# Attention phase of a vision block on one core: scores for the maxima six pairs ahead, maxima turned at step 1, query copies issued in the odd chunks

## The reference, cut to what matters

```
attn_w = softmax(einsum('bhqnd,bhknd->bhnqk', qh, kh) + mask_w)
vw     = einsum('bhnqk,bhknd->bhnqd', attn_w, vh)
attn_h = softmax(einsum('bqwnd,bkwnd->bwnqk', qh, kh) + mask_h)
out    = einsum('bwnqk,bknwd->bqwnd', attn_h, vw)
```

## Time and profile before

| what | value |
|---|---|
| median of 3 runs | 2617.39 us |
| the profiled execution, its own time | 2628.1 us |
| its span | 2626.3 us (1.8 us lie around it) |
| attention phase in the span | about 444 to 1888 us |
| PE / DVE / ACT / POOL busy over the span | 84% / 57% / 47% / 40% |
| mean granted clock of PE | 0.91 of full |
| DMA, mean rate | 133 GB/s |
| mean of one: `exps` / `line_max` / `normalise` (two parts) | 0.54 / 0.62 / 0.51 and 0.63 us |

### The profile page before, as it was taken

How to read it: one execution, slowest core, us unless ns; L and a number is a source line. 1 busy time by engine, 2 the same in 40 slices (tenths; PEclk the granted TensorE clock), 3 DMA queues, 4 the chain that set the end, 5 groups by cost and what they waited for, 6 DMA issues and landing times. The chain is left out here.

```text
span 2626.3 us, 85046 instructions
## 1 busy us (share of the span) xinstructions
PE 2196.2 (84%) x31886; PEld 1742.7 (66%) x31886; DVE 1490.1 (57%) x2350; ACT 1238.4 (47%) x2079; POOL 1061.6 (40%) x1661
## 2 busy tenths in 40 slices
PE   6977515988888898897898989989779984999998
PEld 6977513656666666665666666666579983777777
DVE  3677874656556565554565666666431213677675
ACT  2444531534444444453454544444334554666665
POOL 2344554434444344433444444444312233433433
PEclk9988755989989999887998999999889996999999
DMA  6575536665666666667666666666396753444442
GB/s 106 114 173 154 154 113 143 154 133 132 140 141 143 147 135 143 141 146 166 147 153 146 148 150 149 157 150 161 69 142 124 159 128 101 96 96 94 95 95 68
DMA packets 716326, 348.34 MB, mean 133 GB/s; under 512 B 613481, under 2 KB 675137, under 8 KB 716097
## 3 DMA queue, kind: packets, MB, share of 16 engines
q1 hardware_dynamic: 686993, 314.26, 53.7%
q0 software_dynamic: 28800, 30.58, 4.0%
q10 hardware_dynamic: 304, 0.03, 0.0%
HBM read 105.39 MB, written 102.76 MB: 79 GB/s over the span
## 5 line engine op out<-in xcount | busy, mean ns | idle before, releaser
L693 ACT ACTIVATE att_prob<-att_st_ps 128x448 f32<-128x448 f32 x896 | 487.2, 544 | 674.4 <-PE att_st_ps L585 673.0
L768 DVE TENSOR_REDUCE att_mm<-att_s_ps 128x8 f32<-128x448 f32 x896 | 548.6, 621 | 263.0 <-PE att_s_ps L552 262.0
L598 PEld LDWEIGHTS att_pv_ps<-att_vx,att_prob 128*56 128x56 f32 x14336 | 543.6, 137 | 141.4 <-issue 18.6
L598 PE MATMUL att_pv_ps<-att_vx,att_prob 128*56 128x18 f32 x14336 | 510.8, 205 | 1.8 <-ACT att_prob L693 1.8
L580 PE MATMUL att_st_ps<-att_mvt,att_both 122*56 122x448 bf16 x1792 | 341.0, 376 | 161.9 <-DMA att_mvt<-att_mneg 116.3
L552 PE MATMUL att_s_ps<-att_kx,att_q_unit 120*56 120x448 bf16 x1792 | 335.9, 371 | 5.7 <-DMA att_q_unit<-att_qk_hi 3.2
L585 PE MATMUL att_st_ps<-att_qx,att_k_hi 128*56 128x448 bf16 x1792 | 339.6, 374 | 0.0
L585 PE MATMUL att_st_ps<-att_qx,att_k_lo 128*56 128x448 bf16 x1792 | 336.6, 371 | 0.0
L430 POOL COPY att_vx<-att_vf 56x224 f32<-56x224 f32 x512 | 182.0, 386 | 306.8 <-PE att_pv_ps L598 298.3
L445 POOL DMA_DIRECT2D att_mvt<-att_mneg x256 | 135.8, 535 | 307.8 <-PE att_st_ps L585 232.6
L436 POOL DMA_DIRECT2D att_qx<-att_q_hilo x512 | 245.0, 487 | 26.9 <-DMA att_q_hilo<-att_qk_lo 15.8
(11 more groups left out here) (207 smaller groups left out, 3283.3 us busy)
## 6 DMA issues: line engine op xcount, KB each, us to landing
att_xt<-xn_chunks SPq DMA_DIRECT2D x128, 196.0 KB, 3.6
att_k_hi<-att_qk_hi SPq DMA_DIRECT2D x128, 196.0 KB, 3.8
att_k_lo<-att_qk_lo SPq DMA_DIRECT2D x128, 196.0 KB, 4.1
att_qx<-att_q_hilo POOLq DMA_DIRECT2D x512, 49.0 KB, 3.0
pos_x<-in_x_dram SPq DMA_DIRECT2D x128, 105.0 KB, 3.6
lepe_x<-v_scratch SPq DMA_DIRECT2D x128, 105.0 KB, 3.0
x_scratch<-pos_x SPq DMA_DIRECT2D x128, 98.0 KB
xn_chunks<-pos_xrt SPq DMA_DIRECT2D x16, 784.0 KB, 4.9
```

The lines of the kernel that those rows point to most:

```text
L598: ins = pe.matmul(pv_ps[v % 2][64 * h:64 * h + L, at:at + 18], prob[t % 4][:, 4 * h + a, :], vx[v][:, VW * j + 36 * a + 18 * h:VW * j + 36 ...
L693: act.activation(prob[t % 4][:, :, :], st_ps[t % 2][:, 0:S8].rearrange("p (s q) -> p s q", q=L), ACT.Exp).then_inc(exp_done, 1)
L768: dve.tensor_reduce(mm[v % 2][:, NH * j:NH * j + NH], s_ps[j % 2][:, 0:S8].rearrange("p (s k) -> p s k", k=L), AX.X, ALU.max).then_inc(max ...
```

## The change

Three constants move the work of PE, ACT and DVE by steps: the plain scores run 6 pairs ahead instead of 4, the maxima are turned at step 1 instead of 3, and the two halves of the projection are at steps 0 and 1 instead of 1 and 2. On SP the two `q_hilo` DMAs leave `copies` of the even chunk and follow `keys_and_units` in the odd chunk before. On POOL `fill_max` goes ahead of `fill_k`, on DVE the first `line_max` of a chunk goes ahead of `normalise`. No instruction of a chunk is added or removed, apart from one more wait on SP.

```diff
-        S_EARLY = 4
-        MAXIMA_AT = 3
-        PROJECT_AT = (1, 2)
+        S_EARLY = 6
+        MAXIMA_AT = 1
+        PROJECT_AT = (0, 1)
...
-            def copies(i, w):
+            def queries(i, w):
 
                 wait(sp, qk_low, cnt(i, 2 * w + 1, 2, 2))
                 wait(sp, qx_in[w], unit_count(i, 16 * NH, -16 * NH))
                 sp.dma_start(q_hilo[w][0:C, :], qk_hi[w][0:C, :]).then_inc(hq_in[w], 16)
                 sp.dma_start(q_hilo[w][C:2 * C, :], qk_lo[w][0:C, :]).then_inc(hq_in[w], 16)
+
+            def keys_twice(i, w):
+
+                wait(sp, qk_low, cnt(i, 2 * w + 1, 2, 2))
                 wait(sp, st_done, cnt(i, 2 * w + 1, 7, 7 - 28))
                 for y in range(2):
                     sp.dma_start(k_hi2[w][C * y:C * y + C, :], qk_hi[w][C:2 * C, :]).then_inc(k2_in[w], 16)
...
                     if is_there(*n4):
                         keys_and_units(n4[0], w)
+                        queries(n4[0], w)
                 else:
                     n2 = chunk(i, v, 2)
                     if is_there(*n2):
-                        copies(n2[0], 1 - w)
+                        keys_twice(n2[0], 1 - w)
...
-                if v % 2 and is_there(*n4):
-                    fill_k(pool, n4[0], w, K_POOL, kx_in_sw)
                 if is_there(*n1):
...
                     fill_max(*n1)
+                if v % 2 and is_there(*n4):
+                    fill_k(pool, n4[0], w, K_POOL, kx_in_sw)
...
                 for j in range(PAIRS):
-                    if j == 0 and not is_first(i, v):
-                        normalise(*chunk(i, v, -1))
                     if j < PAIRS - S_EARLY:
                         if is_there(*n1):
                             line_max(*n1, j + S_EARLY)
                     elif is_there(*n2):
                         line_max(*n2, j - (PAIRS - S_EARLY))
+                    if j == 0 and not is_first(i, v):
+                        normalise(*chunk(i, v, -1))
```

More of the change, by code:

```diff
@@ L354, in first @@
                 keys_and_units(i, 0)
-                copies(i, 0)
+                queries(i, 0)
+                keys_twice(i, 0)
                 sp.wait_ge(x_mask, 1)
@@ L367, in first @@
                 keys_and_units(i, 1)
+                queries(i, 1)
                 store_v(i, 2)
```

## The result

| | before | changed |
|---|---|---|
| median, us (lowest to highest) | 2619.28 (2617.33 to 2640.52) | 2506.49 (2504.56 to 2513.52) |
| ratio, with 95% interval | | 0.9556 [0.9519, 0.9593] |
| profiled execution, us / its span | 2628.1 / 2626.3 | 2513.52 / 2511.6 |
| mean granted clock of TensorE | 0.912 | 0.927 |

The medians are of four runs each; the 2617.39 us given for the kernel before at the start is the median without the highest, 2640.52. The change gains 112.8 us; 98 had been forecast (2521 us, range 2486 to 2578). Lines of the changed kernel are 7 higher than before from the attention code on: L587 is the `mvt` matmul that was L580, L592 the keys' matmuls, L559 the scores, L567 `maxima`, L521 the projection, L687 `high`, L693 `negate`, L452 `fill_max`.

The account below looks back on a forecast made before the run. PE's waits for the maxima DMA at even chunk ends were taken as the bound. Columns 72 us plus rows 29, less three late POOL turns at 1.1, gave about 98: median 2519, stated as 2521 us, range 2486 to 2578.

Parts of the forecast that it names:

- What bounds the kernel: PE before the transposed scores: waits for the maxima DMA at the end of even chunks, near 1.8 us each.
- the "issue" waits: PE at row borders: 43.8 us in 11 waits of about 4 us, taken as the hardware loop's turn and staying.
- The working of the new chunk: Step times from the border: negate behind high, 4.05 to 4.31 us; first maxima DMA at 5.07 us, against 6.55 before.
- L552's wait for `neg_done`: PE at step 2: scores pair 1 waits for the negation, adding 0.17 us to each chunk, bounds 0 and 0.5.
- The residual wait of an even chunk: PE's remaining wait for the maxima DMA at even borders: 0.3 us per even chunk in both halves, bounds 0 and 1.2.
- The late turns of POOL: Three column borders where PE lost near 4 us behind a late POOL: 1.1 us of each stays.
- The clock: TensorE's low clock follows border waits: columns counted at 1.00; rows keep a 2.5 us loss per image behind the loop turn.
- The first: Rival: maxima DMA slower as transfers pack closer, 1.2 us per even border instead of 0.3; 2578 us, chance 0.15.
- The third: Rival: q_unit becomes the wait at step 1 of every even chunk; at a 2 us stall 2693 us, chance 0.04.
- The fourth: Rival: the column loop begins to pay at its turn like the row loop; 79 us lost, 2600, chance 0.03.
- The second: Rival, better than forecast: no residual wait and no wait for neg_done; 133 us gained, 2484 us, chance 0.13.
- The query copies: SP's q_hilo DMAs: 392 KB leave the saturated even chunk, counted as no gain.

Follow-up runs that it names:

- the two pairs of runs: Query copies in the even chunk against the odd one: 2509.12 and 2506.49 us with the POOL swap, 2517.68 and 2516.37 us without it.
- the best version: The changed kernel with negate ahead of high on ACT and PE's row loop written out: 2408.06 us, ratio 0.9169 against the kernel before.

## Why the prediction was right, and where it was short

- **What bounds the kernel: right.** The wait for the maxima at the end of even chunks was the cost that the change removes; the turn of the row loop was not, and stayed. The prediction took the "issue" waits for the loop's turn and left 53 us out of the gain for it; the changed kernel has all 13, and writing the loop out removes them. Its guess that two of the "DMA" waits by rows were turns is right too: their places and lengths (4.07 and 4.06 us) say so. The Trainium skill (Runtime: NRT & Kernel Launch, Instruction fetch mechanics) says the same of a taken branch outside the prefetched pages. That it was the fetch inside the turn is only argued; that it is the turn is shown.
- **The working of the new chunk: right.** `negate` behind `high` ended 4.28 us in (worked out 4.31), the DMA left at 5.06 (5.07). The 1.2 us lost behind `high` are real: `negate` ahead of `high` brings 23 us back.
- **The term that was too large: L552's wait for `neg_done`**, taken at 0.17 us for each chunk. In the changed kernel the scores of pair 1 start at 1053.72, 4.33 us in, 0.05 us behind the end of `negate`. PE's own work brings it there at 4.30 (so it is in the run with `negate` first, where nothing holds it: 1409.06 for a border at 1404.76), and not at 4.23: the step with `maxima` and a projection is 1.85 us in the trace (step 1, 1404.92 to 1406.77), where 1.76 had been worked out. So the wait is 0.03 to 0.05 us, not 0.17. With four chunks an image that is some 0.5 us an image, or 15 us over 30 images.
- **The residual wait of an even chunk** was taken at 0.3 us. By columns it is 5.9 us over some 31 even chunks, 0.19. By rows it is 8.8 us in 15 waits, 0.6 each and twice the forecast: there the transfer took 5.2 us in the median of these waits, against the 4.8 that the prediction took from one chunk. The two halves cancel.
- **The late turns of POOL** were to keep 1.1 us each, three by columns. No column border waits over 1.2 us now. POOL still pauses, but in another place, see below. That is 3 us.
- Taken together: column image 37.33 us, forecast 38.0; row image 45.21, forecast 45.6. (0.67 + 0.39) x 15 = 16 us, and with the 3 us of POOL 19; the profiled spans gained 17 us more than the forecast of 98, the medians 15. By columns the 0.67 is 0.5 of `neg_done` and 0.2 of the two even waits. By rows the 0.39 is 0.5 of `neg_done` and 0.3 of the turn (49.5 / 13 = 3.8 us, forecast 4.1), less 0.3 for the even wait. The figure 2521 itself is 2 us above the 2519 of the prediction's own sum, for which it gives no reason.
- **The clock: right for the columns**, 1.00 in every image of that view. PE was busy 41.0 us less in all, with the same instructions. The low clock followed PE's waits at the borders: where they are gone, so is it; by rows, with the loop's turn left, it stayed at 0.95 in the image shown, and it is 1.00 up to 1030 us once the loop is written out.
- **Rivals.** The first, a slower maxima DMA, has a true core: 5.54 against 4.81 us in the row chunk shown, and it cost 0.6 us there. It did not come to 1.2 us per even chunk. The third, `q_unit`, was as near as the prediction put it: in the even chunk by columns that begins at 1403.41 it is issued at 1402.43, lands 2.5 us later and is needed at 1406.22, a cover of 1.3 us. 1.1 us later on SP costs 69 us of waits and as much in time. In the changed kernel it is waited for in 7 places, 5.8 us, of which 3.1 are one wait at the start of the phase. The fourth did not happen: the columns have no wait called "issue", though each image between the first and the last ones turns the loop. The second came true by half.
- **The query copies** were counted at nothing, which was right (1.3 and 2.6 us in the two pairs of runs, within the noise); that they'd be worth 10 to 30 us I came to think only afterwards, and the run refuted it.

Open: how the swap on POOL brings its 9 us, and the 17.8 us at the change from rows to columns, which no run here touched on purpose; the kernel before had 17.2 us there, and the best version still has 17.1, in two waits of 13.0 and 4.1.

## What to carry to other kernels

Find the engine whose wait ends a stage, then follow the chain behind the transfer back through each engine's queue. Here the transfer could leave two steps earlier, but 1.2 us of that were lost because the short instruction on which it hangs stood behind a longer one in the same queue; swapping the two brought a fifth as much again as the whole change. Moving a step earlier uses up the slack of its neighbours, so work out each one's cover in microseconds (here `line_max` on DVE, `q_unit` on SP) before and after. And don't add waits of different kinds together because they stand at the same line: four microseconds of "issue" at every turn of a loop need another cure than a late DMA.

## What was unexpected of the hardware

- **A pause of POOL.** Once in about four images POOL's DMA issue stands for 2.6 to 2.8 us. By columns in the kernel before, it fell between `fill_k` and the maxima, ahead of the DMAs of 1380.12, 1553.86 and 1724.15, and PE paid for it at the border. The first of them:

```profile
1376.21 1.11 POOL L270 DMA_DIRECT2D att_kx<-att_qk_hi  x2 [2.83 <-ACT att_qk_hi L680]
...
1380.12 1.09 POOL L445 DMA_DIRECT2D att_mvt<-att_mneg  x2 [2.80 <-PE att_st_ps L585]
...
1383.75 0.58 PE L580 MATMUL att_st_ps<-att_mvt,att_both 122*56 122x448 bf16 x2 [3.89 <-DMA att_mvt<-att_mneg]
```

In the changed kernel it falls behind the maxima, four times ahead of `fill_q` and twice ahead of `fill_k`. One of the four:

```profile
1297.21 1.10 POOL L452 DMA_DIRECT2D att_mvt<-att_mneg  x2 [2.21 <-ACT att_mneg L693]
...
1301.06 2.42 POOL L443 DMA_DIRECT2D att_qx<-att_q_hilo  x5 [2.75 <-PE att_st_ps L592]
```

From 1377.32, the end of the first `fill_k` row, to 1380.12 POOL issues nothing, though the negation had ended at 1376.39. The bracket names PE, but what `fill_max` waits for from PE, the scores of the chunk before, was done at the border of 1370.58. No run was made on its cause, which stays open.

- **A small transfer beside large ones.** At the borders shown the maxima need 2.41 us in the quiet chunk, 3.40 with 392 KB less than full traffic and 4.8 to 5.5 with the DMA engines near 90% busy. By the Trainium skill (DMA: Bandwidth & Descriptors, Queues, rings and completion order) the engines alternate between queues packet by packet, which alone would let the backlog on SP's queue matter little. The measurement differs: beside the full traffic the transfer takes twice the time of the quiet chunk, and without two of SP's copies a good microsecond less by columns.

- **The clock's share of a wait.** Waits at the borders cost more than their own length, since the work behind them runs at a lower granted clock. How much more differs from run to run: the change removed 74.4 us of waits in all and 41.0 us of busy time, writing the loop out 57.9 and 27.5, `negate` ahead of `high` 15.3 of waits for the maxima and 16.5. That is 0.5 to 1.1 us for each microsecond of wait, and no fixed price. In the kernel before, PE waits 2.12 us until 1438.23, and in the 5 us from there the granted clock is half of full, the lower of its two levels:

```profile
1438.00:1443.00 5.00, 4.77 (x52) 3.11 (x54) 1.80 (x4) 1.09 (x2) 1.80 (x5) 0.50 0.57 154
```
